# One image's 1x1, its whole 3x3, then sixteen rounds of two groups of the preceding image, six of them with the final 1x1

## What is computed

```python
f = relu(einsum('oc,nchw->nohw', Wc, gn(x)) + bc)
gk1 = relu(mean(gn(x), axis=(2, 3)) @ Wc.T + bc)
xm = gn(x).reshape(N, C, 3, H // 3, 3, W // 3).max(axis=(3, 5))
dynW = relu(einsum('oj,ncjkl->nockl', Wck, stack([gk1 * Wkk + bkk, relu(Wc xm + bc)])) + bck)
x1 = x + einsum('oc,nchw->nohw', Wf, conv3x3(f, dynW) + b_ad) + bf
out = x1 + conv3x3(gn(x1), K)          # 32 groups of 16 channels
```

## Time and profile before

| what | value |
|---|---|
| time, median of 3 runs | 3925.79 us (3924.04 to 3929.71) |
| profiled execution, its own time | 3910.82 us |
| its span, first to last instruction | 3909.1 us |
| mean granted TensorE clock | 0.970 |
| PE, DVE, ACT, POOL busy | 91%, 77%, 56%, 25% |
| DMA | 810.21 MB, mean 207 GB/s |

### The profile page before, as it was taken

How to read it: one execution, slowest core, us unless ns; L and a number is a source line. 1 busy time by engine, 2 the same in 40 slices (tenths; PEclk the granted TensorE clock), 3 DMA queues, 4 the chain that set the end, 5 groups by cost and what they waited for, 6 DMA issues and landing times.

```text
span 3909.1 us, 64944 instructions
## 1 busy us (share of the span) xinstructions
PE 3543.0 (91%) x18048; PEld 2728.8 (70%) x18048; DVE 3003.4 (77%) x8020; ACT 2177.4 (56%) x3911; POOL 990.5 (25%) x1036
## 2 busy tenths in 40 slices
PE   5799999999999999998999999999999999999996
PEld 4577776677776777766677767777666777667775
DVE  7788787778787878877787778787777877787853
ACT  4465555665555664556655556655566555566554
POOL 2131222322222322223222123222232131232223
PEclk9899999999999999999999999999999999999998
DMA  5778667777667786668776687866686776778646
GB/s 101 216 217 233 203 187 217 231 228 221 190 197 226 224 231 210 184 193 236 223 229 198 181 227 224 237 212 183 187 249 209 229 211 179 220 220 238 204 112 173
DMA packets 389593, 810.21 MB, mean 207 GB/s; under 512 B 67250, under 2 KB 297012, under 8 KB 376756
## 3 DMA queue, kind: packets, MB, share of 16 engines
q1 hardware_dynamic: 375220, 658.76, 61.2%
q10 hardware_dynamic: 14336, 151.00, 11.0%
HBM read 501.40 MB, written 308.28 MB: 207 GB/s over the span
## 4 chain that ended last, share of the span: by engine, by line
issue 65%; POOL 21%; PE 6%; DVE 3%; DMA 3%; SPq 1%; POOLq 1%; ACT 1%; ACTq 0%; DVEq 0%
POOL hl L410 21%; DMA tb<-x_rows 1%; PE pd L910 1%; PE pb L910 1%; PE pd L911 1%; PE pd L912 1%; PE pb L912 1%; PE pb L911 1%; POOLq L409 1%; DVE bst L636 1%; DVE mx L638 1%; DMA out<-tb 1%; DMA tb<-x 1%; DMA x_rows<-mrow 0%; PE pac L910 0%
## 5 line engine op out<-in xcount | busy, mean ns | idle before, releaser
L410 POOL TENSOR_TENSOR hl<-un,hl 128x384 f16<-128x384 f32 x1024 | 962.9, 942 | 2838.1 <-ACT hl L435 2838.0
L910 PE MATMUL pd<-hl,k_h 128*96 128x384 f16 x3072 | 1043.6, 340 | 220.0 <-POOL hl L410 135.5
L911 PE MATMUL pd<-hl,k_h 128*96 128x384 f16 x3072 | 1036.1, 337 | 0.0
L912 PE MATMUL pd<-hl,k_l 128*96 128x384 f16 x3072 | 1034.5, 337 | 0.0
L821 DVE SCALAR_TENSOR_TENSOR tb<-pd,kout,tb 96x384 f32<-96x384 f32 x1024 | 621.8, 607 | 327.7 <-PE pd L912 321.2
L431 ACT ACTIVATE un<-tb,b_t,s_t 128x384 f32<-128x384 f32 x1024 | 710.2, 694 | 153.8 <-DMA tb<-x_rows 147.1
L435 ACT ACTIVATE hl<-un 128x384 f16<-128x384 f32 x1024 | 538.8, 526 | 298.6 <-PE pd L912 269.5
L910 PEld LDWEIGHTS pd<-hl,k_h 128*96 128x96 f16 x3072 | 388.6, 126 | 418.7 <-issue 192.8
L810 DVE SCALAR_TENSOR_TENSOR x1b<-pac,bfc,xb 128x288 f32<-128x288 f32 (+2 forms) x1408 | 544.1, 430 | 81.9 <-PE pac L912 76.7
L478 ACT ACTIVATE xs<-pb,badc 128x480 fp32r<-128x480 f32 (+1 forms) x160 | 103.5, 647 | 846.0 <-PE pb L912 846.0
L910 PE MATMUL pb<-fh,dynh 128*128 128x480 f32 (+1 forms) x1440 | 553.3, 384 | 8.2 <-DVE dynl L715 8.2
(11 more groups left out here) (107 smaller groups left out, 4014.7 us busy)
## 6 DMA issues: line engine op xcount, KB each, us to landing
x_rows<-x1b SPq DMA_DIRECT2D x128, 1152.0 KB, 13.9
tb<-x_rows SPq DMA_DIRECT2D x128, 1152.0 KB, 9.6
out<-tb ACTq DMA_DIRECT2D x128, 1152.0 KB, 7.9
tb<-x SPq DMA_DIRECT2D x372, 384.0 KB, 9.7
xb<-x SPq DMA_DIRECT2D x124, 720.0 KB, 6.3
xb<-x SPq DMA_DIRECT2D x124, 432.0 KB, 10.6
tb<-x_rows SPq DMA_DIRECT2D x256, 192.0 KB, 10.7
x_rows<-mrow SPq DMA_DIRECT2D x64, 96.0 KB, 10.0
```

The costliest lines, as they stand in the source:

```text
L410: pool.tensor_tensor(hl[:, g % HL_RING, 1, :, 1:W + 1], un[:, g % U_RING], hl[:, g % HL_RING, 0, :, 1:W + 1], ALU.subtract).then_inc(hl_lo, 1)
L910: pe.matmul(acc, high_w, high_x, start=start, stop=False)
L911: pe.matmul(acc, high_w, low_x, start=False, stop=False)
L912: return pe.matmul(acc, low_w, high_x, start=False, stop=stop)
```

## The change

- **x once.** `stage_x` and its second read of x are gone. `xb` has six places: chunks 0 and 1 keep theirs, chunks 2 and 3 alternate between two pairs (`x_slot`). Statistics are taken from `xb` itself: chunks 2 and 3 of the next image during B, chunks 0 and 1 in rounds 3 to 8, after C has freed their places.
- **Order.** A, then at once B without C, then 16 rounds. A round is two groups of image n-1 (`d_pair`); the first six have four of 24 C units each. A C unit is now 384 columns of one chunk: six rows' phase `k` of all eight bands, read with a stride (`y_rows`).
- **Fewer DVE instructions.** `output` takes two groups in one instruction (96x768, from `pb` or `pd`, now two banks each); `residual` has 24 instructions of 384 an image in place of 44.
- **x1 in two places** `x1b` in place of four, each chunk written to DRAM by itself.
- **All DMAs on SP.** `store` moves from ACT's list to SP's. `load_t` of chunks 0 to 2 of image n-1 stands at the start of step n.
- **Chain.** Each link of the statistics stands in a round of its own; `kernel_inputs` and the nine-instruction `dyn_` steps move to the end of the preceding image's rounds, `x1_variances` and the scales into B. `dyn_low` moves into A. Five x units are made ahead in place of four, after the rounds.
- Squares: four of a whole chunk each (2304 elements), in place of twelve.

```diff
-C_AFTER = (2, 4, 6, 8)
-D_FIRST = 13
-LATE = {D_FIRST + 1: (0, 1), D_FIRST + 2: (2, 3)}
+X_SLOTS = 6
+X1_SLOTS = 2
+T_SLOT = [0, 1, 2, 0]
+C_ROUNDS = 6
+C_PER_ROUND = CUNITS // C_ROUNDS
+STATS_IN_B = (2, 3)
+MOMENTS_AT = {3: (0, 0), 4: (0, 1), 6: (1, 0), 7: (1, 1)}
+MAXIMA_AT = {5: 0, 8: 1}
+PREP_MEANS_AT = 8
+PREP_VARIANCES_AT = 10
+PREP_SCALED_AT = 12
...
@@ SP, step @@
+                if d:
+                    for c in range(Q - 1):
+                        load_t(n - 1, c)
+                if more:
+                    for c in STATS_IN_B:
+                        load_x(n + 1, 1 - odd, c)
+                for c in range(2):
+                    write_x1(n, c)
+                    if more and c in STATS_LATE:
+                        load_x(n + 1, 1 - odd, c)
+                if d:
+                    store(n - 1, 0)
+                write_x1(n, 2)
+                if d:
+                    load_t(n - 1, Q - 1)
+                write_x1(n, 3)
+                if d:
+                    store(n - 1, 1)
+                write_means(n)
+                if d:
+                    store(n - 1, 2)
+                    store(n - 1, 3)
...
@@ DVE, step @@
+                for r in range(PAIRS):
+                    if d:
+                        output(n - 1, r)
+                    if r < C_ROUNDS:
+                        for u in range(r * C_PER_ROUND, (r + 1) * C_PER_ROUND):
+                            residual(n, odd, u)
...
+                        if r == PREP_SCALED_AT + 2:
+                            dyn_inputs(n + 1)
+                            for part in DYN_HALVES:
+                                dyn_maxima(n + 1, part)
+                        if r == PREP_SCALED_AT + 3:
+                            for part in DYN_HALVES:
+                                dyn_global(n + 1, part)
+                if more:
+                    for i in range(AHEAD):
+                        x_low(n + 1, 1 - odd, i)
...
@@ PE @@
+            def c_unit(n, u):
+                c, k = divmod(u, OR_)
+                if u >= C_BANKS:
+                    pe.wait_ge(x1_done, n * CUNITS + u - C_BANKS + 1)
...
+            def d_pair(n, p):
+                reached(pe, out_done, n * PAIRS + p - 1)
...
+                    if r == X1_MEANS_AT - 1:
                         x1_group_means(n)
+                    if more:
+                        if r == PREP_VARIANCES_AT - 1:
+                            group_mean(n + 1)
+                        if r == PREP_VARIANCES_AT:
+                            group_variance(n + 1)
+                        if r == PREP_SCALED_AT + 1:
+                            kernel_inputs(n + 1)
```

More of the change, by code:

```diff
@@ L287, in reached, with images @@
                 eng.wait_ge(semaphore, value)
[L289 to L295, removed]
+        def images(eng, step):
+            step(0, 0, d=False)
+            step(1, 1)
+            with nc.Fori(2, N - 2, 2, engines=[eng.engine], hint_back_edge=True) as n:
+                step(n, 0)
+                step(n + 1, 1)
+            step(N - 2, 0)
+            step(N - 1, 1, more=False)
         block = ctx.enter_context(nc.Block())
@@ L383, in _ @@
             images(sp, step)
-            load_t(N - 1, 3)
-            load_t(N - 1, 2)
+            for c in range(Q - 1):
+                load_t(N - 1, c)
+            store(N - 1, 0)
+            load_t(N - 1, Q - 1)
+            for c in range(1, Q):
+                store(N - 1, c)
             for c in range(Q):
@@ L833, in step @@
                 f_low(n, NT - 1)
-                if not d:
-                    dyn_inputs(n, ())
-                    for part in DYN_HALVES:
-                        dyn_maxima(n, part)
-                    for part in DYN_HALVES:
-                        dyn_global(n, part)
-                    dyn_low(n)
-                dyn_steps = [dyn_inputs, dyn_maxima, dyn_maxima, dyn_global, dyn_global]
-                h = 0
-                for g in range(D_FIRST) if d else ():
-                    output(n - 1, g)
-                    if dyn_steps:
-                        dyn_steps.pop(0)(n, DYN_HALVES[g % 2])
-                    if g == DYN_LOW_AT:
-                        dyn_low(n)
-                    if more and g in PREP_AT:
-                        prep_half(n + 1, h)
-                        h += 1
@@ L868, in step @@
-                for g in range(D_FIRST, G):
-                    for c in LATE.get(g, ()):
-                        residual(n, NT - 1, c)
-                    if d:
-                        output(n - 1, g)
-                    if g == AT_X1_SUMS:
+                    if t == SCALES_BEFORE and d:
+                        for i in range(SCALE_STEPS):
+                            x1_scales(n - 1, i)
+                    if more and t <= len(STATS_IN_B):
+                        moments(n + 1, 1 - odd, STATS_IN_B[t - 1])
+                        maxima(n + 1, 1 - odd, STATS_IN_B[t - 1])
@@ L890, in _ @@
             groups()
-            for h in range(2 * PIECES):
-                prep_half(0, h, first=True)
+            for c in range(Q):
+                moments(0, 0, c)
+                maxima(0, 0, c)
             prep_means(0)
@@ L898, in _ @@
                 prep_scaled(0, i)
+            dyn_inputs(0)
+            for part in DYN_HALVES:
+                dyn_maxima(0, part)
+            for part in DYN_HALVES:
+                dyn_global(0, part)
+            for i in range(AHEAD):
+                x_low(0, 0, i)
             images(vec, step)
+            x1_variances(N - 1)
             for i in range(SCALE_STEPS):
                 x1_scales(N - 1, i)
-            for g in range(G):
-                output(N - 1, g)
+            for p in range(PAIRS):
+                output(N - 1, p)
         @block.tensor
```

542 lines of the change are left out of this document (234 added, 308 removed).

## The result

The changed kernel takes **4234.69 us**, the median of 4 runs (4229.39 to 4242.71), against 3924.91 (4 runs, 3911.63 to 3929.71) of the kernel before on the same chip: a ratio of 1.0797, 95% interval 1.0764 to 1.0829. That is 310 us slower, where 234 were forecast. The profiled execution's span is 4229.7.

The account below looks back on a forecast made before the run. PE was taken as near its bound, with DVE deciding where it waits. 135 + 3822 (30 images of 127.4) + 110.4 + 75.5 = 4143, 4145 with the span, and 15 for the median: 4160 us, range 4035 to 4270.

Parts of the forecast that it names:

- three new waits: Per image: PE 3.4 us before pair 10, PE idle 42.4 to 47.8 before A, 3.1 us in B for x.
- The second: End of rounds: PE idle from 42.4 to 47.8 because the next A's first low part comes only after `dyn_global`.
- The smaller ones: Rounds: PE's `group_variance` waits for output 10 and variances until 24.8, `kernel_inputs` for `prep_scaled` until 35.5.
- the two ends: DVE's pair output: between a maximum of its size, 0.86, and two outputs, 1.02; 0.94 taken as the middle.
- the third wait: B: x of chunks 2 and 3 lands late behind store and rows, so tiles 3 and 4 wait, 3.1 us.
- Rival 1: B: x is in time, loads come earlier than SP's queue suggests, the 3.1 goes: 4065 us; chance 0.15.
- Rival 2: Clock falls in the new waits too, 1.4 to 4.2 us more an image: 4200 to 4290; chance 0.17.
- the first case: Whole kernel: the forecast itself, 4160 us, its own range 4090 to 4230; chance 0.55.
- Rival 3: PE is the bound, small products find inputs ready: 3585 us, or 3750 with only the tail wait; chance 0.08.
- rival 4: A tie: the 9 us that go equal the waits that come, 3926 us; chance 0.05.
- some 9 us: Saved per image: the gap of 2.9, half-rate matmuls after it and 4.8 of stall in groups 0 to 12.

Follow-up runs that it names:

- e1: Changed kernel with SP issuing the two x loads behind the first load of rows instead of behind all three: 4066.86 us.
- e5: Changed kernel with chunks 2 and 3 of x read two images ahead, so no x read stands behind the rows: 4046.27 us.
- e2: Changed kernel with PE's small mean and variance products one round later behind their VectorE work, later chain steps moved back too: 3994.61 us.
- e7: Changed kernel with both x read two images ahead and the small chain's wider spacing: 3902.95 us.
- e6: Changed kernel with x read two images ahead and seven of nine taps left out of `dyn_maxima` and `dyn_global`: 3944.72 us.
- e10: Changed kernel with x read two images ahead, old chain spacing, x pieces made in rounds 12 to 15 and `dyn_global` moved into A: 4111.47 us.

## Why the prediction was right, and where it was not

**The direction and the mechanism held.** The forecast was slower with three new waits in named places: before `ps<-mv` (forecast 3.4, measured 3.1 an image), at the end of the rounds (forecast 5.4), and at B's tile 3 for x. The second was 5.0 in the image shown (1301.17 to 1306.14). The smaller ones held too: 2.1 at `ps<-va` against 1.77, 1.2 at the kernel inputs against 0.71. The range held the time. The whole image was 127.4 forecast and 130.2 measured.

**The prices held.** From a pair's output to VectorE's next start are 0.93 (1269.84 to 1270.77, and 1302.10 to 1303.03), where 0.94 was estimated from the two ends; the eighteen take 0.26; the six C rounds of the image shown last from 1227.12 to 1259.50, 32.4 against 32.5.

**Stage by stage.** Rounds to the last product of pair 15: 72.5 forecast, 72.7. From there to A's end the sum has 47.0 - 42.4 = 4.6 to the first low part, and 17.2 from it: 21.8, measured 21.6 with its seam. B 29.7 + 3.1 = 32.8, measured 35.7. So the image is 2.8 longer, and that lies all in B: 30 x 2.8 = 84 us, which is the distance of 4235 from 4160 and a little more.

**The term that was mis-sized is the third wait, and in it the rows.** I let the three chunks of rows end 30.2 after the last store is issued (5.9 + 1.8 + 22.5) and x's chunk 2 land at 34.3. In the 29 images of the trace the last of the rows' packets starts at 32.6, and VectorE has x at 36.4 (35.5 in the image shown, 1172.84 to 1208.36). VectorE's wait is 267.6 / 30 = 8.9 an image in place of 6.5. PE's wait at tile 3 is then 128.8 / 29 = 4.4 where 3.1 were forecast, and behind it stand eight half-rate matmuls, 8 x 0.17 = 1.4, that I had not counted. e1 and e5 show the whole of B's excess, 6.4 us, going with the wait. The prediction's rule (the Trainium skill, "DMA: Bandwidth & Descriptors", section "Queues, rings and completion order") says that each DMA engine takes the descriptors of one issuing engine in ring order. The trace agrees: x's packets begin only when the rows run out, 12.9 us after x's issue. With x behind three chunks of rows there were 8.9 of wait, behind one none.

**Rival 1** (x is in time, 4065) fell as a forecast. e1 and e5 are that case made true by hand, and gave 4067 and 4046. That they meet its number is luck in part: they took 168 and 188 us from 4235, the rival 95 from 4160.

**Rival 2** (the clock falls in the new waits too, 4200 to 4290) came true beside the forecast, and 4235 lies in it, 5 above my own range for the first case. My sum had half-rate matmuls once an image, 0.9 at the start of A. The image shown has them four times, in D behind two waits, in A, and in B above:

```profile
1276.86 0.53 PE L865 MATMUL pd<-hl,k_h 128*96 128x384 f16 x1
1277.17 0.53 PE L866 MATMUL pd<-hl,k_l 128*96 128x384 f16 x1
...
1283.64 0.52 PE L865 MATMUL pb<-hl,k_h 128*96 128x384 f16 x1
1283.96 0.52 PE L866 MATMUL pb<-hl,k_l 128*96 128x384 f16 x1
...
1306.71 0.60 PE L865 MATMUL pac<-xs,wch 128*128 128x480 f32 x1
1307.11 0.60 PE L866 MATMUL pac<-xs,wcl 128*128 128x480 f32 x1
```

By the counts an image loses 14.2 x 0.155 in D, 10.3 x 0.18 in A and 9.5 x 0.17 in B, 5.7 us, where I had 0.9. The kernel before has 13.0 in D, 1.4 in B and 0.3 in A, so the change added 3.4 an image. The section that rival 2 named (the Trainium skill, "TensorE: Matmul & The Clock Gate", section "HAM oscillation — how this bites in real kernels") describes a loop in which every burst behind the wait starts cold. The trace agrees in part: of 30 images 17 have slow matmuls behind both waits in D, 8 behind one, 5 behind none. My argument against it, that groups 13 to 31 keep a clock of 1.00 with 0.8 of waits, was about waits too short to tell.

That rounds still came out as forecast is luck in part. The 30 images of the trace have rounds from 70.0 to 74.5: near 70 where no matmul of D is at half rate, 73 to 74 where twenty are. Mine, 72.5, had none. So the rest of my sum for the rounds was 2.5 too long: 1.3 of it are the waits (3.07, 1.77, 0.82 and 0.71 against 3.4, 2.1, 1.0 and 1.2), and 0.9 the small products themselves (0.24, 0.24, 0.25 and 0.91 in the image shown, against three of 0.5 and one of 1.0); 0.3 stays open. The mean clock cost of 2.2 filled the hole.

**Rival 3** (PE is the bound) and **rival 4** (a tie) fell. But rival 3's condition was a true one: `mv` ready in time. e2 and e7 make it so, and the time comes down by 240 and, with x, by 332. Its price was not: with only the wait at the end of the rounds left it gave 3750, and e7 is at 3903.

**Two slips in the working** changed nothing. The "some 9 us" that the change saves count the slow matmuls of groups 0 to 12 twice, since the stall of 4.8 (24.1 - 19.3) holds them already. And A's own matmuls are 52 x 0.216 + 13 x 0.176 = 13.5, not 14.0.

## What to carry to other kernels

A result that one engine hands to another needs its distance in the consumer's own order: when the items of work between two exchanges grow (pairs of 2.97 in place of groups of 1.5, with maxima behind the output), the same table of places that hid a chain before exposes it, though no engine has more to do. Before pricing a saving, find what runs beside it: here the tail of the rounds and the store-rows-x line were two paths of nearly one length, and 3.6 us taken from one gave 0.3 in the period until the other was moved, and 3.6 after (124.3 in e5, 120.7 in e6). In a queue that keeps its order, put the load that is wanted first ahead of those that are merely ready.

## What was not expected of the hardware

- The clock did not answer alike to like waits. The same two waits, about 3.1 and 1.8 us, stand in all 30 images; in 17 some twenty matmuls of D run at half rate (1.2 GHz in place of 2.4; one image has 27), in 8 some ten, in 5 none. In the image shown ten followed the wait of 1.77 as ten followed that of 3.07, and none those of 0.71 and 0.82. In e10 the same wait of 3.06 has about 17 behind it. One image is therefore no sample of the clock's cost, and the length of a wait does not give it.
- SP's own issue of a DMA grew from 0.58 us to 3.82 and 1.89 for the eighth and ninth of the nine rows DMAs, so x was issued at 1189.92, 11.4 us behind the first. Over 29 images the eighth took 4.7 (3.7 to 5.8), the ninth 1.0. The trace shows no semaphore behind it, and what held it was not tried. It cost nothing here, since x's packets had to wait for the rows for another 12 us and more.
